# Two chunks of the first FFN move into the first attention, and the modulation is computed as rows

## The reference, cut to what matters

```
mod = silu(c) @ wmod            -> sa, ca, ga, sb, cb, gb   (256 each)
h = layernorm(x) * (1 + ca) + sa
x = x + ga * attention(h)       layer 0: causal, with decay; layer 1: full
h = layernorm(x) * (1 + cb) + sb
x = x + gb * ffn(h)
layer 0: ffn = (silu(h @ Wg.T * gs) * (h @ Wu.T * us)) @ Wd.T * ds   (704 inner)
layer 1: ffn = shared FFN (352 inner) + 2 of 8 experts (176 inner) by token
```

## Time and profile before

| engine | busy us | share |
|---|---|---|
| PE matmul | 1399.3 | 91% |
| PE weight load | 591.2 | 39% |
| DVE | 1182.8 | 77% |
| ACT | 1038.1 | 68% |
| POOL | 343.9 | 22% |

### The profile page before, as it was taken

How to read it: one execution, slowest core, us unless ns; L and a number is a source line. 1 busy time by engine, 2 the same in 40 slices (tenths; PEclk the granted TensorE clock), 3 DMA queues, 4 the chain that set the end, 5 groups by cost and what they waited for, 6 DMA issues and landing times. The chain is left out here.

```text
span 1533.5 us, 35240 instructions
## 1 busy us (share of the span) xinstructions
PE 1399.3 (91%) x13320; PEld 591.2 (39%) x13320; DVE 1182.8 (77%) x1528; ACT 1038.1 (68%) x2052; POOL 343.9 (22%) x472
## 2 busy tenths in 40 slices
PE   6988898999899998986999999999999999999988
PEld 5543333333333354441333333333333333247665
DVE  5687897898885044888999979997999789617665
ACT  2345676777788841231899979998999889964432
POOL 2501131200100041223140038201300040145234
PEclk9999999999999998996999999999999999999999
DMA  7821120011000003222100200000000000013454
GB/s 223 150 47 40 47 77 28 30 44 35 1 2 2 1 15 70 49 49 64 81 7 8 55 4 7 7 7 6 7 7 7 7 2 2 12 68 92 143 155 128
DMA packets 56867, 68.51 MB, mean 45 GB/s; under 512 B 9819, under 2 KB 52379, under 8 KB 55963
## 3 DMA queue, kind: packets, MB, share of 16 engines
q1 hardware_dynamic: 53635, 57.87, 14.3%
q0 software_dynamic: 3072, 8.39, 1.8%
HBM read 45.26 MB, written 26.74 MB: 47 GB/s over the span
## 5 line engine op out<-in xcount | busy, mean ns | idle before, releaser
L1800 DVE TENSOR_REDUCE mpart<-psum 128x2 f32<-128x1024 f32 (+2 forms) x832 | 913.2, 1156 | 102.7 <-PE psum L1232 84.1
L1535 ACT ACTIVATE probs<-psum 128x512 f32<-128x512 f32 (+3 forms) x1664 | 846.3, 573 | 163.5 <-PE psum L1263 89.7
L1288 PE MATMUL psum<-probs,v_region 128*17 128x256 f32 (+2 forms) x6144 | 491.6, 392 | 11.8 <-ACT out_sb L1550 8.0
L1232 PE MATMUL psum<-key_region,row_region 50*128 50x512 f16 (+3 forms) x1664 | 320.0, 377 | 61.0 <-DVE mpart L1800 45.1
L1263 PE MATMUL psum<-row_region,key_region 52*128 52x512 f16 (+3 forms) x1664 | 347.4, 376 | 18.2 <-ACT probs L1535 13.0
L1263 PEld LDWEIGHTS psum<-row_region,key_region 52*128 52x128 f16 x1664 | 97.4, 93 | 352.7 <-ACT probs L1535 289.8
L1288 PEld LDWEIGHTS psum<-probs,v_region 128*17 128x17 f32 x6144 | 102.6, 95 | 201.5 <-issue 99.1
L1232 PEld LDWEIGHTS psum<-key_region,row_region 50*128 50x128 f16 x1664 | 94.2, 93 | 165.2 <-DVE mpart L1800 96.5
L1034 POOL TENSOR_SCALAR mp<-mx 128x16 f16<-128x16 f32 x32 | 10.3, 321 | 651.3 <-DVE mx L1811 620.2
L1570 ACT ACTIVATE probs<-psum,gate_s 128x512 f32<-128x512 f32 (+1 forms) x24 | 16.4, 682 | 74.3 <-PE psum L1331 74.3
L1822 DVE SCALAR_TENSOR_TENSOR probs<-psum,up_s,probs 128x512 f32<-128x512 f32 (+1 forms) x24 | 17.9, 747 | 52.7 <-PE psum L1340 43.7
(11 more groups left out here) (192 smaller groups left out, 1326.2 us busy)
## 6 DMA issues: line engine op xcount, KB each, us to landing
parts<-key_region SPq DMA_DIRECT2D x32, 256.0 KB, 3.1
key_region<-parts SPq DMA_DIRECT2D x48, 128.0 KB, 4.4
sorted_x<-in_zero SPq DMA_DIRECT2D x46, 128.0 KB, 2.6
key_region<-sorted_x SPq DMA_DIRECT2D x46, 128.0 KB
sorted_y<-key_region SPq DMA_DIRECT2D x46, 128.0 KB
row_region<-parts SPq DMA_DIRECT2D x144, 32.0 KB
key_region<-in_wmod SPq DMA_DIRECT2D x2, 1536.0 KB, 11.6
x_sb<-in_x SPq DMA_DIRECT2D x4, 512.0 KB, 8.5
```

Of the source, the lines that this page charges most:

```text
L1232: mm = pe.matmul(bank(b + par)[:, 0:w], rows[at, g, hp, r * P:(r + 1) * P], keys[at, g * HP + hp, q * CH:q * CH + w], start=True, stop=not ...
L1288: mm = pe.matmul(psum[32 * h:32 * h + VW, SUM_BANK, lo:hi], v_sb[:, jt, g * HG + h, :], probs[:, (S0[y] + s) % 2, h, lo:hi], start=(jt == ...
L1535: nc.scalar.activation(probs[:, (S0[y] + s) % 2, 2 * hp + par, off:CH], psum[:, e % 3, off:CH], ACT.Exp, scale=SCALES[y]).then_inc(s_p, 1)
L1800: V.tensor_reduce(mpart[:, n % NG, at:at + 2, q:q + 1], psum[:, b:b + 2, 0:w], AX.X, ALU.max).then_inc(drained(*item)[0], 1)
```

## The change

1. The first FFN of chunks 0 and 1 is taken out of the middle stage and put into the first attention by step numbers (`EARLY`, `ffn_in_attention`): its gate and up pairs at steps 62, 65, ..., 77 and 135, 137, ..., 145, down halves at 80, 82 and 147, 149, projections at 88, 90 and 155. Its items hold one of the two attention slots (`held`) until an `hf` item one step later; other items then use the other slot alone.
2. In the attention the silu is a tanh on ACT and two products on DVE, in buffers beside the probabilities (`early_e`, `early_u`).
3. The second layer's first keys and rows are loaded by head group (`load_group`, 14 DMAs) as the last units finish. No maximum pair of the second layer is in the first attention: `FREE_STEP` is the number of its steps.
4. The middle stage has the FFN of chunks 2 and 3 and 66 pairs of the maximum.
5. The modulation lines are computed as rows, four at a time in column groups of 32, copied and transposed.
6. The FFN weights are split a unit earlier; some waits on shared buffers name other items.

```diff
+FREE_STEP = first_step(0, NU)
+EARLY = {0: (62, 3, 80, 88, 90), 1: (135, 2, 147, 155, None)}
...
-            out += work[:first]
+            out += extra[0] + work[:first]
...
-            out += work[first:second]
+            out += extra[1] + work[first:second]
...
+def ffn_in_attention(n, k):
+
+    s = first_step(0, n) + k
+    out = [[], [], []]
+    for tc, (pair, every, down, keys, row) in EARLY.items():
+        for c in range(NC[0]):
+            if s == pair + every * c:
+                out[0].append(("hg", 0, tc, c))
+                out[1].append(("hid", 0, tc, c))
+            if s == pair + every * c + 1:
+                out[0] += [("hf",), ("hh", 0, tc, c)]
+        for z in range(2):
+            if s == down + 2 * z:
+                out[0].append(("dm", 0, tc, z))
+                out[1].append(("dn", 0, tc, z))
+                out[2].append((("sa", "st")[z], 2, tc))
+            if s == down + 2 * z + 1:
+                out[0].append(("hf",))
+        if s == down + 4:
+            out[2].append(("nm", 2, tc))
+        if s == down + 5:
+            out[1].append(("ln", 2, tc))
+        if s == down + 6:
+            out[0].append(("lh", 2, tc))
+        for side, at in [part for part in ((1, keys), (0, row)) if part[1]]:
+            if s == at:
+                out[0].append(("qk", 1, tc, side))
+                out[2].append(("ql", 1, tc, side))
+            if s == at + 1:
+                out[0].append(("hf",))
+    if n > NU - NG and k == 1:
+        out[2] += [("group", n - 1 - (NU - NG))]
...
 def early_blocks():
 
...
-    done = []
-    loaded = [0]
+    done = blocks_in_attention()
+    loaded = [1]
...
+
+    for c in range(NC[0]):
+        out.append(("hg", 0, 2, c))
+        out.extend(tail(0, c))
+        blocks(1 + (c > 1))
+        out.append(("hid", 0, 2, c))
+        if c == 1:
+            loaded[0] = 2
+        blocks(1 + (c > 1))
+        if c in (2, 4):
+            value(c // 2 - 1)
+    for c in range(NC[0]):
+        out.append(("hg", 0, 3, c))
+        blocks(2)
+        out.append(("hid", 0, 3, c))
+        blocks(1)
+        if c == 0:
+            out += [("dn", 0, 2, 0), ("sa", 2, 2)]
+            blocks(2)
+            out.append(("dn", 0, 2, 1))
+            blocks(2)
+            out.append(("st", 2, 2))
+        if c == 1:
+            out.append(("nm", 2, 2))
+            project_rows(1, 1)
+        if c == 2:
+            out.append(("ln", 2, 2))
+        if c == 4:
...
-    out += [("mc", 1), ("mg", 1), ("mr",), ("wo", 0), ("xb", 0, 0), ("xb", 0, 1), ("xb", 0, 2)]
...
-            [("load", 1)] + middle + [("wo", 1)] + [("xb", 1, tc) for tc in range(NCH)],
...
+                    if held is None:
+                        turn[family] = turn.get(family, -1) + 1
+                        b = family[turn[family] % len(family)]
+                    else:
+                        b = 1 - held
+                    if n == 1 and item[0] in ("hg", "dm", "qk"):
+                        held = b
                     count[b] += 1
                     slot[own] = (b, count[b])
                     if b not in used:
                         first_of[own] = n
                     used.add(b)
+                elif item[0] == "hf":
+                    turn[0, 1] = held + 1
+                    held = None
...
+            return s_row[g], 128 * NCH + 96 * i
+
+        def keys_loaded(y, n, q):
+            if y and q == 0:
+                return s_group[n % NG], 96
+            return s_key[q], 96 * (y + 1)
...
+            def load_group(g):
+                sp.wait_ge(*parts_stored(1, 0, 1))
+                sp.wait_ge(*parts_stored(1, 0, 0))
+                sp.wait_ge(s_e, HG * first_step(0, NU - NG + g + 1))
+                for par in range(2):
...
+                        sp.dma_start(keys[lo:lo + HD, g * HP:(g + 1) * HP, 0:CH], src).then_inc(s_group[g], 16)
+                for par in range(2):
+                    sp.dma_start(rows[64 * par:64 * par + C0, g, :, :], a["row_const1"][:, 0:HP, 0:CH]).then_inc(s_row[g], 16)
+                    for k, part in enumerate(ROW_PARTS):
...
                 sp.wait_ge(*parts_stored(y, q, 1))
-                if y and q == 0:
+                if y:
...
-                    col = (0, 1, 3, 4)[i // 2] * D + (i % 2) * P
-                    for k in range(KD):
-                        mm = pe.matmul(bank(b)[:, i:i + 1], wmod[y][:, k, col:col + P],
-                                       cs[:, y * KD + k:y * KD + k + 1], start=(k == 0), stop=(k == KD - 1))
...
+                for c in range(KD):
+                    mm = pe.transpose(bank(b)[:, c * P:(c + 1) * P], mod_lines[:, c * P:(c + 1) * P], ident[:, :])
                 mm.then_inc(filled(*item)[0], 1)
 
...
+                if in_attention(y, tc):
+                    nc.scalar.activation(early_e[k % 2][0:f, :], psum[0:f, bank_of(("hid", y, tc, c)), :], ACT.Tanh,
+                                         scale=gate_h[0:f, c:c + 1]).then_inc(s_sil, 1)
+                    return
...
+                    dve.wait_ge(*filled("md", item[1] - 1))
+                V.tensor_copy(mod_lines, bank(bank_of(item))[:, 0:D]).then_inc(drained(*item)[0], 1)
...
-                V.tensor_copy(modc[:, y, :], bank(b)[:, 0:8]).then_inc(drained(*item)[0], 1)
+                V.tensor_copy(modc[:, y, :].rearrange("p (j c) -> p c j", c=KD),
...
-                t, up = utmp[k % 2][0:f, :], psum[0:f, b + 1, :]
-                if y == 0:
+                t, up = product_of(y, tc, k)[0:f, :], psum[0:f, b + 1, :]
+                if in_attention(y, tc):
+                    e = early_e[k % 2][0:f, :]
+                    link(V.scalar_tensor_tensor(e, e, 1.0, psum[0:f, b, :], ALU.add, ALU.mult))
+                    ins = V.scalar_tensor_tensor(t, up, both_h[0:f, c:c + 1], e, ALU.mult, ALU.mult)
```

More of the change, by code:

```diff
@@ L238, in tail, with blocks_in_attention, place_of @@
             [("st", 2 * y + 1, i)], [("nm", 2 * y + 1, i)], [("ln", 2 * y + 1, i)]][k]
+def ffn_in_attention(n, k):
[29 more added lines that the diff above has]
+        out[2] += [("group", n - 1 - (NU - NG))]
+    free = s - FREE_STEP
+    if free >= 0:
+        out[1] += [b for m in range(NG - 1) for b in pairs_of(1, m) if b[5] == 0][free:free + 1]
+    return out
+def blocks_in_attention():
+    return [b for s in range(first_step(0, NU)) for n, k in [place_of(s)] for part in ffn_in_attention(n, k) for b in part if b[0] == "max"]
+def place_of(s):
+    n = max(m for m in range(NU) if first_step(0, m) <= s)
+    return n, s - first_step(0, n)
 def early_blocks():
     first = [b for n in range(HG) for b in pairs_of(1, n) if b[5] == 0]
+    first = [b for b in first if b not in blocks_in_attention()]
     return first + [b for n in range(HG) for q in range(1, NCH - 1) for b in pairs_of(1, n) if b[5] == q]
@@ L282, in project_rows, with value @@
         out.append(("ql", 1, p, 0))
[L283 to L315, removed]
+    def value(p):
+        out.append(("v", 1, p))
+        blocks(1)
[13 more added lines that the diff above has]
+        out.append(("hid", 0, 3, c))
+        blocks(1)
+        if c == 0:
[10 more added lines that the diff above has]
+        if c == 4:
+            project_keys(2, 1)
     p = NCH - 1
-    loaded[0] = p - 1
     for z in range(2):
@@ L324, in ffn0_walk @@
             out.append(("sa", 2, p))
+            loaded[0] = p
             blocks(2)
     out.append(("st", 2, p))
-    loaded[0] = p
     blocks(1)
@@ L435, in stages @@
     return [prologue_walk(), attention_walk(0, prologue_blocks()),
-            [("load", 1)] + middle + [("wo", 1)] + [("xb", 1, tc) for tc in range(NCH)],
+            [("group", NG - 1), ("keys", 1, 1), ("load", 1)] + middle + [("wo", 1)] + [("xb", 1, tc) for tc in range(NCH)],
             attention_walk(1, done), first, tiles, with_halves(rest)]
-IN_SLOT = ("mc", "mg", "mr", "ln", "qk", "v", "max", "mt", "ft", "bt", "oq", "hg", "dm", "dn", "lg", "px", "tx", "gu", "th", "dw")
+IN_SLOT = ("mc", "md", "mg", "mr", "ln", "qk", "v", "max", "mt", "ft", "bt", "oq", "hg", "dm", "dn", "lg", "px", "tx", "gu", "th", "dw")
 SUM_BANK = 3
@@ L654, in adaln_two_layers @@
         s_key = [sem(f"keys_loaded{q}") for q in range(NCH)]
+        s_group = [sem(f"first_keys_loaded{g}") for g in range(NG)]
+        s_bias = sem("second_projection_biases_loaded")
         s_rows = sem("first_chunk_rows_loaded")
@@ L763, in load_second_projections @@
                     sp.dma_start(dst, a[name].rearrange("(k p) n -> p k n", p=P)).then_inc(s_wraw, 16)
+                for side in range(2):
+                    sp.wait_ge(*drained("qk", 0, NCH - 1, side))
+                sp.dma_start(b_row[:, :], a["b_row1"]).then_inc(s_bias, 16)
+                sp.dma_start(b_col[:, :], a["b_col1"]).then_inc(s_bias, 16)
             def load_ffn(y, i):
```

103 lines of the change are left out of this document (70 added, 33 removed).

## The result

The changed kernel takes 1575.3 us (median of four runs, 1574.4 to 1576.0) where the kernel before, run beside it, took 1539.4 (1535.3 to 1543.5): ratio 1.0225, interval 1.0196 to 1.0254. It is slower by 2.3%, outside the range. The profiled execution has a span of 1573.8 us against 1533.5. That of the kernel before is among its fastest, so the stages add up to 40.3 where the medians differ by 35.9.

The account below looks back on a forecast made before the run. No engine was taken to own the span; PE, DVE and ACT are balanced in attention steps with two pairs. Terms -61 + 39 + 28 - 5 - 4 = -3 gave 1532 on the profiled execution, set to 1535, range 1517 to 1556.

Parts of the forecast that it names:

- (a): Middle stage between the attentions: without two chunks' FFN it takes 141.5 us instead of 202; minus 61.
- (d): Second attention: 12 steps keep one maximum pair where two stood; minus 5, bounds minus 14 and minus 1.
- (b): Chunk 0's FFN in first-attention steps 62 to 91: PE work 30.7 plus stalls 14 less 6; plus 39.
- (c): Chunk 1's FFN in first-attention steps 135 to 156, mostly without maxima; plus 28, bounds plus 22 and plus 37.
- (e): Modulation computed by rows in column groups: saves minus 4, bounds minus 6 and plus 3.
- (f): Costed at nothing: POOL's earlier FFN weight split, the group loads on SP's queue, and tanh in place of silu.
- the relief: Units 9 to 11: about 6 us that 16 steps had waited on DVE, taken off the 14 of stalls.
- the walked step: First-attention step with two pairs and a gate and up pair, summed to 5.0 us of PE.
- C: Rival: held slot in steps 62 to 91 and 135 to 138 makes PE wait in order; 1550 to 1564, chance 0.18.
- F: Rival: the middle stage's new loops, paced by DVE, drop PE's clock to 1.2 GHz; +66, 1600, chance 0.02.
- D: Rival: a maximum taken from the second attention is worth its full 1.16 there; about 1525, chance 0.10.

Follow-up runs that it names:

- e8: Changed kernel with the middle stage's pairs of key chunk 2 allowed only five maxima later; ratio 1.0197 to the kernel before.
- e9: Changed kernel with the edits of e2, e3 and e4 together; 1542.2 us, ratio 1.0042 to the kernel before.
- e4: Changed kernel with 52 maximum pairs in the middle stage instead of 66, the other 14 in the second attention; ratio 1.0105 to the kernel before.
- e2: Changed kernel with the held slot released in its own step and DVE's split right behind its product; ratio 1.0138 to the kernel before.
- e3: Changed kernel with POOL's split of the first FFN's weights seven steps later in unit 8; ratio 1.0204 to the kernel before.
- e13: e9 with 40 maximum pairs in the middle stage instead of 52; ratio 1.0101 to the kernel before.
- e6: Changed kernel with no pair of the first layer's maximum in steps where FFN or projection work holds the slot; ratio 1.0215 to the kernel before.
- e1: Kernel before with the row-product modulation alone, no FFN work or pair moved; ratio 0.9976 to the kernel before.
- e12: e1 with 41 maximum pairs in the middle stage instead of 52; 1534.7 us, ratio 0.9957 to the kernel before.

## Why the prediction was wrong, by its own steps

Forecast 1535; the profiled change is +40.3, forecast -3. The miss of 43 is 14 in (a), 8 in (d), 9 in (b), 7 in (c), 1.5 in (e) and 3.4 in (f); nothing large cancelled. The terms:

(a), -61 forecast, -46.9 measured. The step charged 46 maxima to the two loops and filled DVE to 0.95; the loops' window shows 73.7 of 91.6, 0.80, for 45. So 18 us of DVE's idle time stood beside 14 of PE's, where the step allowed 4 for slots that fill late; that they come from the two engines handing slots to each other is my reading, no run took them apart. The loops took 91.6, not 82 + 1.3. The end was given two maxima fewer and 58.2; it has 36 before and after and took 63.9, that is the 60.5 of before and 3 more for keys that had not landed (e8). With 52 pairs -61 comes out (e9), but that is luck for the step, which had said it for 66. This is the step that failed most, with (d), its counterpart: 14 pairs were bought for 10 to 15 us.

(d), -5 forecast, +2.9 measured. Without units 4 and 12 the second attention fell by 2.7 us, for 12 pairs fewer in them: 0.2 a pair, or 0.3 without the first unit, where 0.13 had been read from a whole unit. The rest of the 5, from 0.7 a pair "near a unit's start", is not there. Units 4 and 12 grew by 3.1 and 2.5 us, for with fewer pairs two transposes of a maximum wait for POOL, busy with token rows (2.54 and 1.66 us). The sum had no term for that. All six kernels with 66 pairs have both waits, and e4 and e9 with 52 have neither.

(b), +39 forecast, +48.1 measured. The mechanism was right, PE's work plus stalls; both sizes were low. PE is busy 37.8 us more in units 9 to 11, where 30.7 were charged, and idle 10.3 more, where 14 less 6 were. By place, the pair steps 62 to 79 took 24.5 more (forecast 21.4), the down halves 8.8 (10.8), the projections and what goes with them 14.8 (12.8). That is 3 over the 45 before the relief, and the relief of 6 from DVE's waits is not to be seen. DVE's split stood last in its step (e2, 2 x 1.76), and products after the second such idle ran at half clock. With the order mended it is 40.3 (e9), 1.3 over the forecast. Two slips in the working did no harm: the walked step adds up to 4.8 as listed, and to 5.0 with the scores of its first half, and 2 us for 12 items on top of 31 are 55, not 56.

(c), +28 forecast, +35.3 measured: down halves 8.0 for 7.9, pairs 3.3 each for 2.4 (3.0 at full clock, e3), and in all 4.3 of half clock in unit 15, which the profiles of e3, e4 and e13 do not have and those of e2, e6, e8 and e9 have in part.

(e), -4 forecast, -2.5; mechanism right (e1).

(f), nothing forecast, +3.4 in unit 8. POOL's 22% of the span was the wrong thing to look at: 1.2 us are one DVE instruction that POOL's earlier split held up, 2.2 the clock at the chunk change (e3). The tanh was rightly free.

Of the rivals, C had the right side and a part of the mechanism, PE waiting in order. It set the decision at 78 for (b) and (c), and had the middle at -55; measured are 83.4 and -46.9. Its own time, 1550 to 1564, was passed too, and (b) stayed under its 56. But the single slot (e6) is not it; the order of DVE's list is, for a tenth, and the rest is PE's time. F was priced at 0.02 for the wrong place: the loops kept 0.98, and short spells came into the attention. D, a pair worth 1.16 in the second attention, is refuted by e4.

What explains that even e9 gains nothing: between the attentions PE was busy 175 of 202 us, in the first attention 398 of 444. In e9 PE is busy 59 us less in the middle and 72.7 more in the first attention, and idle 2 less and 4.5 more. So the work came out at more than it had cost, and hardly any idle time was filled. That a move between two stages so full cannot pay is argued from these sums; no run shows a better place for it.

e12 is the fastest of all kernels run: 1534.7 us, 0.9957 (0.9931 to 0.9983) of the kernel before and 2.6% below the changed kernel, 0.2% below e1, which its interval does not separate.

## What to carry to other kernels

Before work is moved, add up the same engine's busy time in both stages: if both are nearly full, only the idle time that it lands in counts, and that is to be read from a row at the place, not from a mean. Count work with a due date apart from work that is free: filling gaps with maxima helped until the partner engine was full, and it left the due ones where they were. In a queue that is served in order, put what empties a shared slot right behind what it reads.

## What was not expected of the hardware

A short idle of PE can cost about twice its length. After 1.76 us the granted clock was 0.64 over the next 8 us, and the step lost 3.6 (e2). Ten us before, the same idle left the clock at 1.00 and cost 1.7; no run shows what parts the two. Such spells come and go between executions of one kernel: ten runs of e9 lie between 1538.6 us (mean clock 0.979) and 1549.3 (0.970). So one unit of one profile can differ by 4 us between kernels that are alike there, as unit 15 does (47.8 us at clock 1.00, 52.1 at 0.90).

An instruction of POOL can hold one of DVE that shares no buffer with it: a norm of 0.40 us took 1.61 beside POOL's split of 1.59 (e3), in six of six profiles.

A table load of 1283 ns parts exponential and silu, none parts exponential and tanh, in twelve changes each way.
